# Expert rows weighed at eviction and summed by adding gathers instead of multiply-adds

## What is computed

```
scores = softmax(flat @ router_w.T + router_bias)
topk_scores, topk_idx = top_k(scores, 4)
topk_scores = topk_scores / topk_scores.sum(-1)
h   = silu(flat @ gate_w[e]) * (flat @ up_w[e])        # every expert e, hidden width 128
sel = (h @ down_w[e])[topk_idx]                         # four rows of 256 for each token
out = (sel * topk_scores[:, :, None]).sum(1) + shared(flat)
```

## Time and profile before

| | us |
|---|---|
| time, median of 3 runs | 960.7 (958.2 to 963.5) |
| profiled execution, span from first to last instruction | 958.8 |
| PE busy in the span | 799.9 |
| DVE busy | 503.9 |
| POOL busy | 421.5 |
| ACT busy | 315.6 |
| L568, gathers of results, 64 times on POOL | 64.3 |
| L575, subtraction of maxima, 32 times on POOL | 72.2 |
| L1198, multiply-adds, 64 times on DVE | 57.4 |
| L590, gathers of rows, 95 times on POOL | 91.1 |

### The profile page before, as it was taken

The page is one execution under the profiler, slowest core; times in us unless marked ns, Lnnn a source line. Parts: engine busy times, 40 slices in busy tenths (PEclk is TensorE's granted clock), DMA queues, the critical chain, the costliest instruction groups (busy, mean ns, idle before and its releaser), DMA issues. The chain is left out here.

```text
span 958.8 us, 15942 instructions
## 1 busy us (share of the span) xinstructions
PE 799.9 (83%) x4041; PEld 595.9 (62%) x4043; DVE 503.9 (53%) x1598; ACT 315.6 (33%) x896; POOL 421.5 (44%) x463
## 2 busy tenths in 40 slices
PE   4799999585699599999994789988693299999995
PEld 3688888343366366777762567777572167777773
DVE  2788886542133565555543799999552123333331
ACT  1355554011122144444431344444330033333331
POOL 1243442033767354554543776667442233333321
PEclk8899999598899799999998799999785599999998
DMA  7333233402020144444453235545896211111000
GB/s 193 139 114 112 88 122 105 117 13 16 13 22 0 36 132 134 140 138 140 136 126 97 72 108 170 179 174 126 108 126 134 65 34 38 48 33 45 25 23 2
DMA packets 57926, 87.30 MB, mean 91 GB/s; under 512 B 22073, under 2 KB 43033, under 8 KB 56476
## 3 DMA queue, kind: packets, MB, share of 16 engines
q1 hardware_dynamic: 43996, 57.35, 23.3%
q0 software_dynamic: 13600, 27.33, 11.0%
q10 hardware_dynamic: 288, 2.10, 0.6%
HBM read 67.04 MB, written 22.44 MB: 93 GB/s over the span
## 5 line engine op out<-in xcount | busy, mean ns | idle before, releaser
L590 POOL DMA_INDIRECT U<-normed,idx x95 | 91.1, 959 | 98.1 <-issue 64.8
L575 POOL TENSOR_TENSOR U<-U,mx 128x1232 f32<-128x1232 f32 x32 | 72.2, 2256 | 100.9 <-DVE mx L1207 100.6
L1039 PE MATMUL bank<-R,U 128*128 x380 | 103.7, 396 | 5.9 <-issue 3.9
L757 ACT ACTIVATE X<-bank,U 128x128 f32<-128x128 f32 x184 | 50.1, 383 | 127.3 <-PE bank L1076 127.3
L1092 PE MATMUL bank<-R,X 128*128 x184 | 84.2, 601 | 0.0
L1103 PE MATMUL bank<-R,X 128*128 x368 | 83.3, 379 | 1.0 <-ACT X L757 1.0
L1103 PEld LDWEIGHTS bank<-R,X 128*128 128x128 f32 x368 | 69.8, 190 | 20.1 <-issue 11.7
L1039 PEld LDWEIGHTS bank<-R,U 128*128 128x128 f32 x380 | 65.4, 192 | 19.3 <-issue 11.7
L568 POOL DMA_INDIRECT U<-expert_out,slot_cur x64 | 64.3, 1005 | 22.4 <-issue 15.2
L507 POOL DMA_INDIRECT table<-tok_cur,slot_cur x64 | 61.6, 962 | 26.5 <-issue 22.0
L623 POOL DMA_INDIRECT out<-U,idx_out x23 | 23.4, 1019 | 106.9 <-DVE idx L1118 67.2
(11 more groups left out here) (187 smaller groups left out, 1681.4 us busy)
## 6 DMA issues: line engine op xcount, KB each, us to landing
R<-in_w SPq DMA_DIRECT2D x16, 1024.0 KB
R<-in_gu SPq DMA_DIRECT2D x8, 1024.0 KB, 5.5
expert_out<-U SPq DMA_DIRECT2D x48, 128.0 KB
expert_out<-xr SPq DMA_DIRECT2D x47, 128.0 KB
normed<-xr SPq DMA_DIRECT2D x32, 128.0 KB
R<-in_down SPq DMA_DIRECT2D x8, 512.0 KB, 3.7
x<-X SPq DMA_DIRECT2D x16, 128.0 KB
X<-in_x ACTq DMA_DIRECT2D x1, 1536.0 KB, 8.7
```

What stands on the lines that cost most here:

```text
L575: pool.tensor_tensor(s3, s3, mx[u][:, :].unsqueeze(2).to_broadcast([P, H, S2]), ALU.subtract).then_inc(T["sub"], 1)
L590: pool.indirect_dma_start(xg0[u], None, xn_d[0], bass.IndirectOffsetOnAxis(idx[u][:, :], 0)).then_inc(EX[0]["gath"][u], 16)
L757: ins = act.activation(hT1[:, c, :], bank[5 + g][:, (c % 4) * P:(c % 4 + 1) * P], ACT.Relu, bias=b1_of[u][:, c:c + 1])
L1039: mm = pe.matmul(bank[2 + u][:, 0:2 * F0], xgT0[u][:, c, :], gu_w[:, c, bass.ds(e, 1), :].rearrange("p a n -> p (a n)"), start=(c == 0), s ...
```

## The change

The results are weighed where they leave PSUM, and the sums are made by DMA.

- In layer 0's attention DVE also subtracts the largest score from all 32 scores (`by_expert`, one 128x32 instruction a tile), ACT takes their exponential, and DVE multiplies them with the inverse sum. SP writes these 32 weights behind each row of `normed0`, whose rows become 1152 bytes wide (DW = 288 words). The gathers of rows wait for that write.
- The gather in layer 0's experts therefore brings with each row its weight for every expert. DVE picks the column of the tile's expert out of it into `w_slot` (a 128x1 copy at an address from a register; four registers are loaded every fourth tile), and the eviction L1501 becomes a multiplication by it. The buffer `t0_` goes, `th0` is written in place.
- In layer 1's attention `yg`, the slot copies and `combine` go. POOL gathers straight into `x` with addition. The four additions into a tile wait for one another, one a step: in `step(t)` j = 3 of tile t + 5, j = 2 of t + 6, j = 1 of t + 7, j = 0 of t + 8, in this order. POOL's steps are all written out, from t = -8.
- DVE's statistics of tile t + 3 wait for the fourth addition.
- The places of some buffers in SBUF move.

```diff
 HEAD0 = [P * c // S2 for c in range(PC)]
-UW = 11600
-PICKED_END = 10690
-VF_BACK = 632
+UW = 11664
+PICKED_END = 10832
+VF_BACK = 492
+DW = D + E0
...
         table_d = [nc.dram_tensor(f"table{l}", (P * (c + 1), 1), I32).ap() for l, c in enumerate((ROWS0, ROWS1))]
-        xn_d = [nc.dram_tensor(f"normed{l}", (N, D), F32).ap() for l in range(2)]
+        xn_d = [nc.dram_tensor(f"normed{l}", (N, w), F32).ap() for l, w in enumerate((DW, D))]
         x3_d = nc.dram_tensor("x3", (N, D), F32).ap()
...
-        o = temp_at + 4 * FS
-        es, o = cut(U, o, (NT,))
-        er, o = cut(U, o, (NT,))
+        es = sb("es", [P, NT])[:, :]
+        er = sb("er", [P, NT])[:, :]
+        w_slot = [sb(f"w_slot{i}", [P, 1]) for i in range(4)]
         rk = sb("rk", [P, NT * TOPK])[:, :]
...
                     phase_barrier(sp, 1)
-                sp.dma_start(rows_in[t], xn_d[0][t * P:(t + 1) * P, :]).then_inc(SH["rows"][t], 16)
+                sp.dma_start(rows_in[t], xn_d[0][t * P:(t + 1) * P, 0:D]).then_inc(SH["rows"][t], 16)
             with sp.Fori(1, NT // 4) as k:
...
                     sp.wait_ge(SH["xt_mm"], t - 3)
-                    sp.dma_start(rows_in[u], xn_d[0][bass.ds(t * P, P), :]).then_inc(SH["rows"][u], 16)
+                    sp.dma_start(rows_in[u], xn_d[0][bass.ds(t * P, P), 0:D]).then_inc(SH["rows"][u], 16)
+            sp.wait_ge(RTL[0]["weighing"], 3)
+            sp.dma_start(xn_d[0].rearrange("(t p) w -> p t w", p=P)[:, :, D:DW], by_expert).then_inc(
+                table_init, 16)
             phase_barrier(sp, 2)
...
                             scatter(a)
-                    if l == 1 and on(t, 5):
-                        u = par(5)
-                        need(pool, TL["x_comb"], t + 4)
-                        pool.tensor_copy(slot_cur[u][:, :], slot[:, bass.ds((t + 5) * TOPK, TOPK)]).then_inc(
-                            TL["slots"], 1)
-                        wait_apart(pool, TL["slots"], t + 6)
-                        for j in range(TOPK):
+                    for j in reversed(range(TOPK if l == 1 else 0)):
+                        i = t + 8 - j
+                        if 0 <= i < NT:
+                            if j:
+                                pool.wait_ge(TL[f"sum{j - 1}"], 16 * (i + 1))
+                            need(pool, TL[f"sum{j}"], 16 * i)
                             pool.indirect_dma_start(
-                                yg[:, u * TOPK + j, :], None, y_d,
-                                bass.IndirectOffsetOnAxis(slot_cur[u][:, j:j + 1], 0)).then_inc(TL["gath"][u], 16)
+                                x[:, i, :], None, y_d,
+                                bass.IndirectOffsetOnAxis(slot[:, i * TOPK + j:i * TOPK + j + 1], 0),
+                                compute_op=ALU.add).then_inc(TL[f"sum{j}"], 16)
                     if on(t, 2):
...
-                attention_steps(pool, step)
-                if l == 1:
+                if l == 0:
+                    attention_steps(pool, step)
+                else:
+                    for t in range(-8, NT + 3):
+                        place[0] = t % 2
+                        step(t)
                     scatter(NT - 1)
...
             routing(pool, 0)
+            pool.wait_ge(table_init, 16 * 5)
...
             act.activation(wgt[:, :], wgt[:, :], ACT.Exp).then_inc(RTL[0]["exp"], 1)
+            rows = by_expert.rearrange("p t e -> p (t e)")
+            act.activation(rows, rows, ACT.Exp).then_inc(RTL[0]["exp"], 1)
...
-                def combine(t, j):
-                    u = par(4) if j < 2 else par(3)
-                    xt_ = x[:, bass.ds(t, 1), :].rearrange("p a n -> p (a n)")
-                    if j == 0:
-                        dve.wait_ge(TL["gath"][u], landed(t, 2, TOPK))
-                    else:
-                        dve.wait_ge(TL["summing"], 3 * t + j)
-                    dve.scalar_tensor_tensor(
-                        out=xt_, in0=yg[:, u * TOPK + j, :], scalar=wgt[:, bass.ds(t * TOPK + j, 1)],
-                        in1=xt_, op0=ALU.mult, op1=ALU.add).then_inc(
-                            TL["x_comb"] if j == TOPK - 1 else TL["summing"], 1)
                 def maxima(n, u, g):
...
                                           ALU.add).then_inc(T["x"], 1)
-                    if l == 1 and on(t, 3):
-                        combine(t + 3, 2)
                     if on(t, -2):
...
                         dve.max_index(i8[w][:, :], m8[w][:, :], lg[:, 0:ne]).then_inc(RT["ix"], 1)
-                    if l == 1 and on(t, 3):
-                        combine(t + 3, 3)
                     if on(t, -1):
...
                         if l == 1:
-                            wait_apart(dve, TL["x_comb"], t + 4)
+                            dve.wait_ge(TL["sum3"], 16 * (t + 4))
                         row_stats(T, par(3), t + 3)
...
+                        if isinstance(t, int) and t == 2:
+                            dve.wait_ge(table_init, 64)
+                        dve.tensor_scalar(by_expert[:, bass.ds(t - 2, 1), :].rearrange("p a e -> p (a e)"), lg[:, :],
+                                          m8[w][:, 0:1], None, ALU.subtract)
                         dve.tensor_scalar(wgt[:, bass.ds((t - 2) * TOPK, TOPK)], m8[w][:, 0:TOPK], m8[w][:, 0:1],
...
                                     ins.then_inc(T["copied"], 1)
-                                elif l == 1 and on(t, 4):
-                                    combine(t + 4, g)
                         maxima(n + 2, u, 0)
-                    elif l == 1 and on(t, 4):
-                        for j in range(2):
-                            combine(t + 4, j)
                 attention_steps(dve, step)
...
                 dve.wait_ge(RTL[0]["weighing"], 2)
-                dve.tensor_tensor(w3, w3, er.unsqueeze(2).to_broadcast([P, NT, TOPK]), ALU.mult)
+                dve.wait_ge(RTL[0]["exp"], 2)
+                dve.tensor_tensor(by_expert, by_expert, er.unsqueeze(2).to_broadcast([P, NT, E0]), ALU.mult).then_inc(
+                    RTL[0]["weighing"], 1)
...
                     values(1, s * B * PC // 4, (s + 1) * B * PC // 4)
+                if on(s, 2, TILES0):
+                    if par(2, 4) == 0:
+                        dve.reg_load(dve_experts, plan_e[0:1, bass.ds(s + 2, 4)])
+                    e = expert(dve, dve_experts, par(2, 4), E0)
+                    dve.wait_ge(X0["xt_mm"], s + 3)
+                    dve.tensor_copy(w_slot[par(2, 4)][:, :], xg0[par(2, 4)][:, bass.ds(D + e, 1)])
                 if on(s, 6, TILES0) and not (isinstance(s, int) and s < -2):
-                    need(dve, X0["xt_mm"], s + 3)
                     column(idx[par(6, 4)], s + 6, X0["idx"])
...
                     dve.wait_ge(X0["th"], s + 3)
-                    dve.scalar_tensor_tensor(out=t0_[u], in0=th0[u], scalar=1.0, in1=bank[2 + u][:, 0:F0],
+                    dve.scalar_tensor_tensor(out=th0[u], in0=th0[u], scalar=1.0, in1=bank[2 + u][:, 0:F0],
                                              op0=ALU.add, op1=ALU.mult).then_inc(X0["act"], 1)
                     dve.wait_ge(X0["act"], s + 3)
-                    dve.scalar_tensor_tensor(out=h0[u], in0=t0_[u], scalar=0.5, in1=bank[2 + u][:, F0:2 * F0],
+                    dve.scalar_tensor_tensor(out=h0[u], in0=th0[u], scalar=0.5, in1=bank[2 + u][:, F0:2 * F0],
                                              op0=ALU.mult, op1=ALU.mult).then_inc(X0["h"], 1)
...
                     need(dve, X0["out"][par(0, 4)], 16 * (s // 4))
-                    dve.tensor_copy(y0[par(0, 4)], bank[6 + u][:, 0:D]).then_inc(X0["y"], 1)
+                    dve.tensor_scalar(y0[par(0, 4)], bank[6 + u][:, 0:D], w_slot[par(0, 4)][:, :], None,
+                                      ALU.mult).then_inc(X0["y"], 1)
             experts0_steps(dve, experts0)
```

More of the change, by code:

```diff
@@ L136, in build @@
         pT, o = cut(U, o, (PC, P))
-        yg, o = cut(U, o, (2 * TOPK, D))
+        o += 2 * TOPK * D
         k_sb, o2 = cut(U, o - 2 * TOPK * D, (B * S2,))
+        by_expert = cut(U, o2, (NT, E0))[0]
         zeros, o2 = cut(U, o2, (ROWS0,), I32)
@@ L168, in build @@
         o = temp_at
-        xg0, xgT0, h0, hT0, y0, th0, t0_ = [], [], [], [], [], [], []
+        xg0, xgT0, h0, hT0, y0, th0 = [], [], [], [], [], []
         for i in range(2):
-            for lst, shape in ((xgT0, (KC, P)), (h0, (F0,)), (hT0, (P,)), (y0, (D,)), (th0, (F0,)), (t0_, (F0,))):
+            for lst, shape in ((xgT0, (KC, P)), (h0, (F0,)), (hT0, (P,)), (y0, (D,)), (th0, (F0,))):
                 v, o = cut(U, o, shape)
                 lst.append(v)
-        o = max(o, temp_at + 4 * FS + 2 * NT)
+        o = temp_at + 4 * FS
         for i in range(4):
-            v, o = cut(U, o, (D,))
+            v, o = cut(U, o, (DW,))
             xg0.append(v)
@@ L308, in build @@
         KV = Sems("kv")
-        AT, ATL = Sems("at"), [Sems(f"at{l}", gath=2) for l in range(2)]
+        AT, ATL = Sems("at"), [Sems(f"at{l}") for l in range(2)]
```

(2 more changed lines are left out.)

3 lines of the change are left out of this document (2 added, 1 removed).

## The result

The changed kernel takes 986.7 us (median of 4 runs, 982.7 to 988.7) where the kernel before takes 961.8 on the same chip (958.2 to 963.5): 1.0243 times as long, with a 95% interval of 1.0206 to 1.0281. The profiled execution has a span of 983.1 us against 958.8, so 24.3 us are to be found. The forecast was 952, and its range ended at 982.

What follows compares the result with a forecast made beforehand. DVE, busy 11.20 of 11.35 us, was taken to bound layer 1's attention steps, PE those of layer 0. Start + 10, steps - 17.3, tail - 4, layer 0's experts + 3 gave -8.3 us: 960.7 to 952, range 943 to 982.

Steps and rivals of the forecast that it cites:

- The price of an adding gather at issue: POOL in layer 1's attention: 0.96 us to issue, as a plain gather; bounds 0.19 and 1.92 us.
- Rival B: Adding gathers cost POOL more at issue, making it the bound: 1001 us at 1.92 each, near 975 at 1.44; chance 0.20.
- the cycle of 8.9 us: POOL's work and waits in a layer 1 attention step after the change, with gathers of 0.96 us at issue.
- The chain at the start: Start of layer 1's attention: four linked additions, landing 3.2 us each, make the first power about 10 us later.
- rival C: Adding gathers land slowly, lengthening the start and stopping POOL in each step: 990 us at 10 us a landing; chance 0.13.
- The steps: Layer 1's attention: DVE relieved, PE sets 9.3 us a step, eleven intervals fall from 117.6 to 100.3, gain 17.3 us.
- The tail: Layer 1's attention, last `sub` to PE after the barrier, 91.0 us: gain 4 us, bounds 9 gained and 5 lost.
- The wait of 7.15 us for the last tile: Tail of layer 1's attention: DVE's wait at 681.87 for the last tile's gathers, forecast to go by up to 7.15 us.
- The experts of layer 0: Layer 0's experts: later `idx` copies and wider rows delay gathers PE waits for; 3 us lost, bounds 0 and 10.
- the mechanism named: Layer 0's experts: weight copy and register loads precede the copy of `idx`, on which the gather hangs; at most 0.05 us a tile.
- The small parts: Layer 0's attention and the write of weights beside the rows, before the first gather of rows: no cost taken.

Runs made afterwards that it cites:

- plain_gathers: Changed kernel with plain gathers in place of the adding ones, sums and residual left out, same order and waits; ratio 0.996 to the kernel before.
- half_rows: Changed kernel storing and adding only the first 128 of the 256 columns of a result; ratio 1.023 to the kernel before.
- after_loads_early: Changed kernel with layer 1's expert weight loads issued three experts earlier; ratio 1.032 to the kernel before, its profiled run 1.016.
- adds_after_sub: Kernel before with all four multiply-adds of a tile at the end of a step, none on POOL's `sub`; ratio 0.995 to the kernel before.
- after_scatters_last: Changed kernel with the scatters of the row table moved behind `sub` in POOL's order; ratio 1.016 to the kernel before.
- before_scatters_last: Kernel before with the scatters of the row table moved behind `sub` in POOL's order; ratio 1.000 to the kernel before.

## Why the prediction was wrong, point by point

**The price of an adding gather at issue** is the step that failed. It was taken as 0.96 us, "what a plain one takes here", with bounds of 0.19 and 1.92. It is 1.56, and plain_gathers shows that without it 26.5 us go (11.3 at the start, 15.2 in the steps): more than the whole loss of 24.3. Rival B named this mechanism and its price list was about right. At 0.6 us more it gives 8.4 at the start and 4.4 for each 0.1 beyond the first, 22, in the steps; measured are 11.3 and 15.2. The start cost more than listed since the list counts the 14 issues before the first power and not the eight between it and the first `sub`. The steps cost less since the cycle of 8.9 us holds waits that a busy POOL no longer has: with gathers of 1.56 it would be 11.3, but the 0.44 us for `ve` are gone and the gap in front of the first gather is 0.12 and not 0.31, which leaves the 10.7 measured. The nearest row was a plain gather, and the choice of its value had no other ground than that nearness; the argument against B in the prediction (that 0.96 us is the same for gathers of any row) speaks of row sizes, and half_rows confirms just that for adding ones.

**The chain at the start** was right: + 10 were forecast with cheap gathers, and plain_gathers has + 8.9. The first link took 4.1 us (524.01 to 528.10; 3.0 in plain_gathers), the median landing of adding gathers is 4.8 us in the loop (plain ones there 4.5), against the 3.2 assumed and within 2.8 to 5.6; with gathers of 1.85 us between issues that is covered from the third step on, so rival C's landing decided nothing. In after_loads_early it did: + 11.2 us at the start.

**The steps**: DVE without multiply-adds was forecast at 6.9 us and is 6.54; PE was to set 9.3 us with cheap gathers and does (9.43, and eleven steps in 97.6 against 100.3). Both halves were right, and POOL's price overruled them. What the reading missed is that the 11.3 us of before were not DVE's work: adds_after_sub takes 12 us off them with the same work.

**The tail**: 4 us of gain were forecast, there was none. The wait of 7.15 us for the last tile did go, as named; a stall of the same size took its place, on ACT:

```profile
702.52 0.38 ACT L707 ACTIVATE xrT<-bank 128x256 f32<-128x256 f32 x1 [8.71 <-remote]
703.22 0.38 ACT L711 ACTIVATE oT<-bank 128x256 f32<-128x256 f32 x1 [0.31 <-remote]
```

PE, DVE and, with 9.75 us, `sub` at 705.11 wait behind it. "Remote" names no instruction of the program; one packet of each of the two instruction queues lies between 693 and 704, so that ACT waited for its own instructions is a guess. The stall is no accident of one run: ACT stands 7.0 to 10.0 us for "remote" in six of the seven experiments with POOL's steps written out, also where the loads were moved away (9.83 in after_loads_early); only after_scatters_last has none. The step "up to 7.15 us and 2 of the clock go" was wrong in taking one wait for the bound of the stretch: when it goes, another takes its place, here and in before_scatters_last. What the stretch is bound by stays open.

**The experts of layer 0**: + 3 forecast with 0 to 10 as bounds, + 6.1 measured. Kernels with the old and the new layer 0 lie at least 2.6 us apart and 5.6 by their lowest. Leaving out the mechanism named, the pick ahead of `idx`, takes 2 to 4 us off the ring's share; the wider row, doubted too, carries none. The rest is open. The Trainium skill's rule (SBUF — State Buffer, Who interferes with whom) that a DVE `copy` and GpSimd may wait out each other did not show: the 128x1 copy of the weight has a mean of 149 ns in the ring, the copy of `idx` the same 149.

**The small parts** were right: POOL's first gather of rows moved by 0.9 us.

## What to carry to other kernels

Before work moves to a queue that another engine must feed, price the issue and not the transfer: the accumulating form of an indirect DMA cost 0.6 us more at POOL than the plain one, and POOL, 8.9 of 9.3 us full by the forecast's own count, had no room for it. Where two engines block each other, look at which instruction falls on the block before taking work off; moving two instructions by half a step brought the steps 12 of the 17 us that removing all four did. And after each gain look for what the stretch behind it waits for: here the tail took back 10 of 12 us until the scatters and loads were moved as well.

## What the runs showed of the hardware

An adding gather of 128 rows takes POOL 1.56 us at issue, with rows of 512 as of 1024 bytes; a plain one of 1024 takes 0.97 in plain_gathers and 1.00 in the kernel before. It also costs the DMA engines more. Queue q0 from 600 to 640 us, changed kernel, with the landing of its gathers:

```profile
q0 software_dynamic: 1994, 1.81, 31.7%
...
X<-expert_out,slot POOLq DMA_INDIRECT x15, 4.8
```

In the kernel before that queue moved 2.10 MB in 768 packets with 14.2% of the engines: a megabyte by adding took 2.6 times the engine time (31.7 / 1.81 against 14.2 / 2.10). In plain_gathers, with the same waits and steps of 9.4 us, it moved 2.34 MB in 860 packets with 20.1%, against which it is 2.0 times. A scalar-tensor-tensor of 128x256 took 0.41 us with a constant and 0.48 with a column as scalar. Scatters of 128 words of 4 bytes landed 12.0 us after issue (median of 16 in adds_after_sub), and with no other traffic the barrier behind them opened 13.9 us after the last one.
